# Edge features turned on the host, and gathers that read their row numbers in the table

## The chip, the cores and the metric

One core of a Trainium2 chip runs the whole program. The metric is device time in microseconds, the median of several runs. Times of single stretches come from one profiled execution.

## The reference, cut to what matters

Four graph layers over 3125 nodes and 100000 edges (sorted by destination), each followed by a layernorm. The change touches the second layer alone, its sum over the edges:

```python
src, dst = (edge_index[0], edge_index[1])
m_input = jnp.concatenate([node_states[src], node_states[dst], edge_rel_emb], axis=-1)
h = jax.nn.relu(m_input @ W1 + b1)
messages = jax.nn.relu(h @ W2 + b2)
agg = jax.ops.segment_sum(messages, dst, num_segments=node_states.shape[0])
updated = node_states + jax.nn.relu(agg @ Wn + bn)
```

`edge_rel_emb` is `edge_attr_64`, 64 numbers an edge.

## The kernel before

The edge loop takes the edges in 196 blocks of 512 (`BLK`, four columns of 128, `J` = 4), with four buffer slots (`SLOTS`). Ahead of it, fourteen steps project the node rows by the two halves of `W1` and store them in HBM as `xa_d` and `xb_d` (SP, lines 564 to 570; DVE copies them out at line 2029, into `proj(n)`).

For a block, in slot `v`:

- **POOL** (`gather`, line 730) issues four indirect DMAs, one for each 128 edges, that fetch rows of `xa_d` into `z_e[v]`. Each waits for its row numbers in a small table `idx` (semaphore `idx_ready`) and for the slot to be free (`z_ready` of the block four before). The first four blocks are written out, the rest run in a loop, the last block has a tail of its own (`last_gather`, line 739, two DMAs).
- **DVE** copies the row numbers of the block four ahead from the resident table `src_idx` to `idx` (`gather_index`, line 2013), adds a finished window of sums into the node sums (`add_window`), writes two one-hot tables for the block three ahead (`block_start`: line 2044 into the columns beside the features, line 2045 into `oh_e`), and adds the bias to the messages (`add_bias`, line 2049).
- **SP** (`edge_loads`, line 586) loads the features, 512 rows of 64, edges on partitions, into `ec` (`features`, line 553, after `ec_used` of two blocks before), and 24 rows of `xb_d` into `w_e` (line 590).
- **PE** turns features and one-hot columns (`inputs_t`, line 1027, four transposes), turns the gathered rows and adds the product of `w_e` and the turned inputs onto them (`hidden_t`, lines 1041 and 1045, which ends in `z_ready`), multiplies by `W2` (`messages`, line 1052) and sums messages by destination (`sum_nodes`, line 1061). In step `v` the order is: hidden of `v+1`, sums of `v-1`, inputs of `v+2`, messages of `v`.
- **ACT** copies the turned inputs out of PSUM into the one buffer `ec_t` (`inputs_out`, line 1478) and does the two relus (lines 1484 and 1488).

In five stretches of the loop the update of finished nodes is woven in (`blocks`, line 388), and in most blocks PE also adds a part of the next layer's sums (`partial`, line 1102).

## Time and profile before

| what | us |
| --- | --- |
| runs (three): median, lowest, highest | 1679.42, 1676.05, 1679.87 |
| the profiled execution, whole | 1675.27 |
| its span, first to last instruction | 1673.1 |
| PE busy | 1451.8 |
| POOL busy | 763.0 |
| DVE busy | 754.3 |
| ACT busy | 667.5 |
| the gathers in the edge loop (line 735), from and to | 489.7 to 1466.6 |

The time outside the span, 2.2 us, is the same work for any version. Busy times of different engines overlap; what a stage costs is read from the engine that the others wait for in that stage. Rows of the trace name the line, the engine, the tiles written and read, the time and, in brackets, the idle time ahead and what ended it.

### The profile page before, as it was taken

To read this page: it belongs to the slowest core of one execution; us is meant where nothing else is said; L and a number is where in the kernel's file an instruction comes from. 1 tells how busy PE (TensorE), PEld (TensorE's weight loads), DVE (VectorE), ACT (ScalarE), POOL (GpSimd) and SP (SyncE) were. 2 spreads that over 40 slices of the span, in tenths; PEclk is the share of its full clock that TensorE was granted. 3 is DMA by queue.
4 is the path that set the end of the run, shared out by engine and by line. 5 is a ranking of instruction groups with operands and counts; after the bars stand their busy time and mean duration, and the time that the engine had idled before them with its cause. 6 is when DMAs were issued, how large, how long until landed. Compare 5 with 4: busy or idle time off the path is not lost.

```text
span 1673.1 us, 30324 instructions
## 1 busy us (share of the span) xinstructions
PE 1451.8 (87%) x9336; PEld 1032.7 (62%) x9336; DVE 754.3 (45%) x2856; ACT 667.5 (40%) x1243; POOL 763.0 (46%) x806
## 2 busy tenths in 40 slices
PE   4899999999958777888989988998898889877997
PEld 3556666555556566666766766766666667654554
DVE  8799999513333222333243333333432343345445
ACT  6766666410023333443345334433443344331113
POOL 3000000000027777777777777777777777721000
PEclk9999999999978999999999998999899989988999
DMA  2000000020053333333333333333333333300001
GB/s 69 1 1 1 2 2 1 8 61 1 0 147 95 83 81 81 79 89 84 79 85 87 80 82 84 85 82 81 84 88 79 81 86 83 82 21 1 0 1 39
DMA packets 158120, 95.18 MB, mean 57 GB/s; under 512 B 119959, under 2 KB 143422, under 8 KB 158030
## 3 DMA queue, kind: packets, MB, share of 16 engines
q0 software_dynamic: 25024, 51.25, 12.0%
q1 hardware_dynamic: 133006, 42.78, 10.5%
q8 instruction: 50, 0.82, 0.2%
q14 instruction: 40, 0.33, 0.1%
HBM read 87.44 MB, written 6.52 MB: 56 GB/s over the span
## 4 chain that ended last, share of the span: by engine, by line
PE 31%; POOL 13%; DMA 11%; issue 9%; DVE 5%; ACT 1%; DVEq 1%; SPq 1%; POOLq 0%; ACTq 0%
POOL arena L735 13%; DMA arena<-x_w1a,idx 9%; PE ps L1167 6%; PE ps L1052 6%; PE ps L1061 5%; PE ps L1045 4%; PE ps L1041 3%; PE ps L1033 3%; PE ps L1102 2%; PE ps L1151 1%; DVE arena L2049 1%; DVE idx L2016 1%; DVEq L336 1%; DMA x_w1b<-arena 1%; DVE stats L2063 1%
## 5 line engine op out<-in xcount | busy, mean ns | idle before, releaser
L735 POOL DMA_INDIRECT arena<-x_w1a,idx x780 | 737.7, 946 | 713.3 <-issue 674.2
L1478 ACT ACTIVATE arena<-ps 88x512 f32<-88x512 f32 x196 | 116.2, 593 | 480.3 <-PE ps L1033 470.0
L1061 PEld LDWEIGHTS ps<-arena 128*128 128x128 f32 x1568 | 208.6, 196 | 111.5 <-issue 72.8
L2049 DVE TENSOR_TENSOR arena<-ps,bias_b 128x512 f32<-128x512 f32 x196 | 135.5, 691 | 208.0 <-PE ps L1052 208.0
L2044 DVE TENSOR_TENSOR arena<-win_i,late 128x96 f32<-128x96 f32 x196 | 50.8, 259 | 391.8 <-PE ps L1061 378.8
L1041 PE MATMUL ps<-ident_f,arena 128*128 128x128 f32 x784 | 130.1, 290 | 107.3 <-DMA arena<-x_w1a,idx 106.4
L1052 PE MATMUL ps<-w_c,arena 128*128 128x128 f32 x1568 | 222.6, 288 | 0.0
L1303 ACT ACTIVATE adj<-ps 128x300 f32 x392 | 171.0, 451 | 108.3 <-PE ps L800 103.8
L1045 PE MATMUL ps<-arena 88*128 88x512 f32 x392 | 208.0, 612 | 3.1 <-ACT arena L1478 3.1
L1052 PEld LDWEIGHTS ps<-w_c,arena 128*128 128x128 f32 x1568 | 205.9, 205 | 0.3
L1061 PE MATMUL ps<-arena 128*128 128x24 f32 x1568 | 197.9, 264 | 4.9 <-ACT arena L1488 1.4
L1041 PEld LDWEIGHTS ps<-ident_f,arena 128*128 128x128 f32 x784 | 91.1, 146 | 157.6 <-DMA arena<-x_w1a,idx 150.6
L795 PE MATMUL ps<-arena 128*128 128x300 bf16 x784 | 165.8, 294 | 25.2 <-DVE arena L1764 21.6
L1764 DVE TENSOR_SCALAR arena<-late,arena 128x300 bf16<-128x300 int16 x784 | 179.5, 292 | 0.0
L1484 ACT ACTIVATE arena<-ps,cols 128x512 f32<-128x512 f32 x196 | 134.6, 687 | 73.0 <-PE ps L1052 73.0
L844 PE MATMUL ps<-arena,adj 128*128 128x385 bf16 x625 | 151.7, 333 | 2.7 <-issue 2.7
L1033 PE MATMUL ps<-ident_f,arena 128*88 128x128 f32 x784 | 128.9, 290 | 25.7 <-DMA arena<-in_edge_attr 15.4
L795 PEld LDWEIGHTS ps<-arena 128*128 128x128 bf16 x784 | 85.0, 114 | 73.6 <-DVE arena L1764 26.1
L1488 ACT ACTIVATE arena<-arena 128x512 f32<-128x512 f32 x196 | 123.4, 630 | 11.2 <-DVE arena L2049 4.1
L800 PE MATMUL ps<-adj,ident_h 128*128 x392 | 122.9, 314 | 5.4 <-ACT adj L1303 3.8
L1167 PE MATMUL ps<-adj,arena 128*128 128x512 bf16 (+1 forms) x525 | 110.1, 364 | 8.8 <-DVE arena L2339 5.1
L1033 PEld LDWEIGHTS ps<-ident_f,arena 128*88 128x88 f32 x784 | 96.1, 152 | 28.6 <-DMA arena<-in_edge_attr 16.0
(205 smaller groups left out, 1406.7 us busy)
## 6 DMA issues: line engine op xcount, KB each, us to landing
arena<-in_edge_attr SPq DMA_DIRECT2D x196, 128.0 KB, 2.3
arena<-x_w1a,idx POOLq DMA_INDIRECT x782
arena<-x_w1b SPq DMA_DIRECT2D x196, 12.0 KB
x_spill<-arena SPq DMA_DIRECT2D x1, 1600.0 KB, 8.6
x_w1a<-arena SPq DMA_DIRECT2D x6, 256.0 KB, 2.3
x_w1b<-arena SPq DMA_DIRECT2D x6, 256.0 KB, 2.7
arena<-x_spill SPq DMA_DIRECT2D x6, 256.0 KB, 3.4
out_x<-arena SPq DMA_DIRECT2D x3, 512.0 KB
```

Source lines behind the costliest of these rows:

```text
L735: pool.indirect_dma_start(out=z_e[v][:, j * D:(j + 1) * D], out_offset=None, in_=xa_d[:, :], in_offset=bass.IndirectOffsetOnAxis(ap=idx[:, ...
L795: last = pe.matmul(ps[:, bank, 0:NT * WIN_A], oh_src[v][:, :, j], oh_dst[v][:, j, :], start=(j == 2 * h), stop=False)
L844: last = pe.matmul(ps[:, c1_bank(k), 0:3 * D + 1], adj[:, u, k * P:(k + 1) * P], mov_x[:, u, 0:3 * D + 1], start=(u == 0), stop=(u == NT - 1))
L1033: last = pe.transpose(ps[0:KE, 0, j * P:(j + 1) * P], ec[v % 2][:, j, :], ident_f[:, :])
L1041: pe.matmul(z_t[:, j * P:(j + 1) * P], z_e[v][:, j * P:(j + 1) * P], ident_f[:, :], is_transpose=True, start=(j == 0), stop=False)
L1045: pe.matmul(z_t, w_e[v % 2][0:KE, :], ec_t[0:KE, :], start=False, stop=True).then_inc(z_ready[v], 1)
L1052: last = pe.matmul(ps[:, 5, j * P:(j + 1) * P], h_t[:, j * P:(j + 1) * P], w_c[:, :], start=True, stop=True)
L1061: last = pe.matmul(ps[:, WIN_BANK[v % 2], 0:WIN], msg[:, j * P:(j + 1) * P], oh_e[v][:, j, :], start=(j == 0), stop=(j == J - 1))
L1167: last = pe.matmul(dst_bank(u), parts[q][:, k, :], adj[:, k, k0 * P:(k0 + nt) * P], start=((k, q) == (NT - 1, 0)), stop=(u != NC - 2 and ( ...
L1303: act.activation(adj[:, :, bass.ds(b, WIN_A)], ps[:, q % 4, 0:NT * WIN_A].rearrange("p (k w) -> p k w", w=WIN_A), ACT.Copy).then_inc(adj_w ...
L1764: last = dve.tensor_scalar(oh_dst[v][:, j, :], iota_c, comb[:, bass.ds(s, 1), j], None, ALU.is_equal)
L2049: dve.tensor_tensor(msg.rearrange("p (j d) -> p j d", d=D), bank(5, J), over(bias_b, J), ALU.add).then_inc(m_sum[v], 1)
```

## The change

The features come from the host turned (`attr_turned`, 64 rows of one number per edge), so that SP loads them straight into the rows of the matmul operand `ec_t`, of which there are now two. Into the 24 rows below, SP loads each edge's destination number, the same in all 24 rows (`dst_numbers`, int32), and DVE makes the one-hot rows there in place (`onehot_turned`): one compare of 24 x 512 against a column that holds the first node of the block plus the row's number (`first_nodes`). `inputs_t` on PE, `inputs_out` on ACT, and the one-hot columns of `block_start` on DVE are gone. `gather_index` and `idx` are gone too: POOL's 782 gathers are written out one by one, with no loop, and read their row numbers in `src_idx`. The features now wait for `z_ready` of two blocks before. In the first steps, DVE makes `first_nodes` where it copied four groups of row numbers.

```diff
         def features(i, v):
             e0 = (SLOTS * i + v) * BLK
-            passed(sp, ec_used, i, v, back=2)
-            sp.dma_start(ec[v % 2][:, :, 0:R],
-                         t["edge_attr_64"][bass.ds(e0, BLK), :].rearrange("(j p) f -> p j f", p=P)
+            passed(sp, z_ready, i, v, back=2)
+            sp.dma_start(ec_t[v % 2][R:KE, :].bitcast(I32),
+                         t["dst_numbers"][bass.ds(e0, BLK)].rearrange("(a e) -> a e", a=1).broadcast_to([WIN, BLK])
                          ).then_inc(ec_loaded[v], 16)
+            sp.dma_start(ec_t[v % 2][0:R, :], t["attr_turned"][:, bass.ds(e0, BLK)]).then_inc(ec_loaded[v], 16)
...
         def gather(i, v):
-            passed(pool, idx_ready, i, v)
             passed(pool, z_ready, i, v, back=SLOTS)
             pool.sem_inc(gather_mark, 1)
             for j in range(J):
                 pool.indirect_dma_start(out=z_e[v][:, j * D:(j + 1) * D], out_offset=None, in_=xa_d[:, :],
-                                        in_offset=bass.IndirectOffsetOnAxis(ap=idx[:, v, j:j + 1], axis=0)
+                                        in_offset=bass.IndirectOffsetOnAxis(ap=src_idx[:, SLOTS * i + v, j:j + 1], axis=0)
                                         ).then_inc(g_loaded[v], 16)
...
-            for v in range(SLOTS):
-                gather(0, v)
-            with pool.Fori(1, NB // SLOTS - 1) as i:
-                for v in range(SLOTS):
-                    gather(i, v)
-            for v in range(SLOTS - 1):
-                gather(NB // SLOTS - 1, v)
+            pool.wait_ge(words_moved, 48)
+            for n in range(NB - 1):
+                gather(n // SLOTS, n % SLOTS)
             last_gather(NB // SLOTS - 1, SLOTS - 1)
...
         def hidden_t(i, v):
...
-            passed(pe, ect_out, i, v)
+            passed(pe, ec_onehot, i, v)
             passed(pe, w_loaded, i, v, by=16)
-            pe.matmul(z_t, w_e[v % 2][0:KE, :], ec_t[0:KE, :], start=False, stop=True
+            pe.matmul(z_t, w_e[v % 2][0:KE, :], ec_t[v % 2][0:KE, :], start=False, stop=True
                       ).then_inc(z_ready[v], 1)
...
-            dve.tensor_tensor(ec[v % 2][:, :, R:KE], w, rel, ALU.is_equal).then_inc(ec_onehot[v], 1)
             dve.tensor_tensor(oh_e[v], w, rel, ALU.is_equal).then_inc(oh_e_ready[v], 1)
+
+        def onehot_turned(i, v):
+            passed(dve, ec_loaded, i, v, by=32)
+            rows = ec_t[v % 2][R:KE, :]
+            dve.tensor_scalar(rows, rows.bitcast(I32), first_nodes[:, bass.ds(SLOTS * i + v, 1)], None,
+                              ALU.is_equal).then_inc(ec_onehot[v], 1)
...
-        def step(i, v, b=None, left=3, first=False):
-
-            if left >= 3:
-                gather_index(*at(i, v + SLOTS))
+        def step(i, v, b=None, left=3):
+
             if b is not None:
                 add_window(*at(i, v - 2), b)
             if left >= 3:
-                block_start(*at(i, v + 3), first)
+                block_start(*at(i, v + 3))
+            if left >= 2:
+                onehot_turned(*at(i, v + 2))
             add_bias(i, v)
```

## Rows read from the trace of the kernel before

**Rows 1.** The page's chain that ended last, shares of the span by line.
```profile
POOL arena L735 13%; DMA arena<-x_w1a,idx 9%; PE ps L1167 6%; PE ps L1052 6%; PE ps L1061 5%; PE ps L1045 4%; PE ps L1041 3%; PE ps L1033 3%; PE ps L1102 2%; PE ps L1151 1%; DVE arena L2049 1%; DVE idx L2016 1%; DVEq L336 1%; DMA x_w1b<-arena 1%; DVE stats L2063 1%
```

**Rows 2.** Line 735: count, duration in ns (least/median/most), first and last start in us.
```profile
L735 POOL DMA_INDIRECT arena<-x_w1a,idx x780: 938/944/1217, 489.7 to 1466.6; - x195
```

**Rows 3.** Timeline of POOL, loop's start: start, duration in us, idle before in brackets.
```profile
489.67 1.13 POOL L735 DMA_INDIRECT arena<-x_w1a,idx  x1 [473.06 <-issue]
491.11 0.94 POOL L735 DMA_INDIRECT arena<-x_w1a,idx  x1 [0.31 <-issue]
...
511.51 0.94 POOL L735 DMA_INDIRECT arena<-x_w1a,idx  x1 [1.99 <-PE ps L1045]
...
517.61 0.94 POOL L735 DMA_INDIRECT arena<-x_w1a,idx  x1 [1.41 <-DVE idx L2016]
```

**Rows 4.** Waits, 540 to 1470 us: us in total, times, longest.
```profile
PE ps L1041 <- DMA arena<-x_w1a,idx: 106.4, 116, 1.8
```

**Rows 5.** The page's costliest groups: busy us, mean ns of one, idle before.
```profile
L1033 PE MATMUL ps<-ident_f,arena 128*88 128x128 f32 x784 | 128.9, 290 | 25.7 <-DMA arena<-in_edge_attr 15.4
```

**Rows 6.** The chain in order of time, ahead of the loop: start, us, what.
```profile
476.03 0.59 SPq L556
...
476.66 0.51 SPq L556
...
477.74 2.33 DMA x_w1a<-arena
```

**Rows 7.** Groups of DVE by line and shape: busy us, mean ns of one.
```profile
L1874 DVE TENSOR_SCALAR arena<-arena,mv,rstd 128x128 f32<-128x128 f32 x25 | 6.8, 340 | 0.1
L2008 DVE TENSOR_TENSOR arena<-arena 128x1024 f32<-128x1024 f32 x3 | 3.7, 1225 | 0.1
L1715 DVE TENSOR_SCALAR arena<-arena 128x784 int32<-128x784 int32 x1 | 0.6, 554 | 0.0
...
L2454 DVE TENSOR_SCALAR late<-ident_f 128x128 f32<-128x128 f32 x1 | 0.2, 219 | 0.0
```

**Rows 8.** Timeline, two copies of row numbers and the gathers that they meet.
```profile
930.21 0.95 POOL L735 DMA_INDIRECT arena<-x_w1a,idx  x1 [0.30 <-issue]
930.74 0.41 DVE L2016 COPY idx<-late 128x4 int32 x1 [1.21 <-issue]
...
1362.69 0.94 POOL L735 DMA_INDIRECT arena<-x_w1a,idx  x1 [0.30 <-issue]
...
1363.16 0.16 DVE L2016 COPY idx<-late 128x4 int32<-128x4 int32 x1
```

**Rows 9.** Timeline, a two-input operation of DVE and the longest gather of the loop.
```profile
1373.71 0.68 DVE L2117 TENSOR_TENSOR arena<-arena 128x512 bf16<-128x512 f32 x1
1373.99 1.22 POOL L735 DMA_INDIRECT arena<-x_w1a,idx  x1 [0.30 <-issue]
```

**Rows 10.** Timeline, a block's last gather, its transposes, the one-hot after them; two blocks.
```profile
871.26 0.95 POOL L735 DMA_INDIRECT arena<-x_w1a,idx  x1 [0.30 <-issue]
...
873.77 0.66 PE L1041 MATMUL ps<-ident_f,arena 128*128 128x128 f32 x4 [1.33 <-DMA arena<-x_w1a,idx]
...
876.13 0.26 DVE L2044 TENSOR_TENSOR arena<-win_i,late 128x96 f32<-128x96 f32 x1 [0.18 <-PE ps L1061]
876.26 0.95 POOL L735 DMA_INDIRECT arena<-x_w1a,idx  x1 [0.30 <-DVE idx L2016]
...
1001.43 0.94 POOL L735 DMA_INDIRECT arena<-x_w1a,idx  x1 [0.30 <-issue]
...
1004.24 0.66 PE L1041 MATMUL ps<-ident_f,arena 128*128 128x128 f32 x4 [0.32 <-DMA arena<-x_w1a,idx]
...
1006.71 0.26 DVE L2044 TENSOR_TENSOR arena<-win_i,late 128x96 f32<-128x96 f32 x1 [2.76 <-PE ps L1061]
```

**Rows 11.** Busy us by engine in two stretches of the loop, then granted clock, DMA.
```profile
540.00:600.00 60.00, 44.78 (x316) 36.30 (x315) 16.73 (x63) 24.15 (x38) 45.37 (x48) 1.00 0.34 84
...
1034.00:1044.00 10.00, 6.41 (x32) 5.63 (x32) 4.68 (x20) 3.19 (x6) 7.57 (x8) 0.67 0.49 121
```

More of the change, by code:

```diff
@@ L94, in build @@
         drel = late[:, J * (NB + 1):LATE].rearrange("p (s j) -> p s j", j=J)
-        base_row = sb("base_row", [1, NB], I32)
+        node_numbers = sb("node_numbers", [P, NB], I32)
+        base_row = node_numbers[0:1, :]
+        first_nodes = node_numbers[R:R + WIN, :].bitcast(F32)
         w_a = sb("w_a", [P, D], F32)
@@ L161, in edge @@
             return arena[:, a:a + n]
-        ec = [edge(J * KE * u, J * KE).rearrange("p (j f) -> p j f", j=J) for u in range(2)]
-        o = 2 * J * KE
+        ec_t = [edge(512 * u, 512) for u in range(2)]
+        o = 1024
         z_e = [edge(o + 512 * v, 512) for v in range(SLOTS)]
         h_t = edge(o + 2048, 512)
-        msg = edge(o + 2560, 512)
-        assert o + 3072 <= 3776
-        ec_t = edge(8000, 512)
+        msg = edge(8000, 512)
         w_e = [edge(9280 + 128 * u, 128) for u in range(2)]
@@ L261, in build @@
         ec_onehot = [sem(f"ec_onehot{v}") for v in range(SLOTS)]
-        ec_used = [sem(f"ec_used{v}") for v in range(SLOTS)]
         w_loaded = [sem(f"w_loaded{v}") for v in range(SLOTS)]
         oh_e_ready = [sem(f"oh_e_ready{v}") for v in range(SLOTS)]
-        ect_out = [sem(f"ect_out{v}") for v in range(SLOTS)]
         z_ready = [sem(f"z_ready{v}") for v in range(SLOTS)]
@@ L275, in build @@
         g_loaded = [sem(f"g_loaded{v}") for v in range(SLOTS)]
-        idx_ready = [sem(f"idx_ready{v}") for v in range(SLOTS)]
         gather_mark = sem("gather_mark")
@@ L1025, in _ @@
             pe.wait_ge(loads[6], 80)
-            def inputs_t(i, v, first=False):
-                passed(pe, ec_loaded, i, v, by=16)
-                if first:
-                    passed(pe, ec_onehot, i, v)
-                    passed(pe, ect_out, i, v, back=1)
-                for j in range(J):
-                    last = pe.transpose(ps[0:KE, 0, j * P:(j + 1) * P], ec[v % 2][:, j, :], ident_f[:, :])
-                last.then_inc(ec_used[v], 1)
             def hidden_t(i, v):
@@ L1071, in step @@
                     sum_nodes(*at(i, v - 1))
-                if left >= 2:
-                    inputs_t(*at(i, v + 2), first)
                 messages(i, v, first)
@@ L1197, in _ @@
             with pe.Else():
-                inputs_t(0, 0, first=True)
-                inputs_t(0, 1, first=True)
                 hidden_t(0, 0)
@@ L1473, in _, with hidden_relu @@
             act.wait_ge(loads[6], 80)
-            def inputs_out(i, v):
-                passed(act, ec_used, i, v)
-                passed(act, z_ready, i, v, back=1)
-                act.activation(ec_t[0:KE, :], ps[0:KE, 0, :], ACT.Copy).then_inc(ect_out[v], 1)
-            def hidden_relu(i, v, first=False):
-                if first:
-                    passed(act, z_ready, i, v)
+            def hidden_relu(i, v):
+                passed(act, z_ready, i, v)
                 passed(act, m_ready, i, v, back=1)
@@ L1490, in step @@
             def step(i, v, left=2):
-                if left >= 2:
-                    inputs_out(*at(i, v + 2))
                 if left >= 1:
@@ L1643, in _ @@
             with act.Else():
-                inputs_out(0, 0)
-                inputs_out(0, 1)
-                hidden_relu(0, 0, first=True)
+                hidden_relu(0, 0)
                 for v in range(SLOTS + 1):
@@ L2011, in _ @@
             phase_end(dve, 4)
-            def gather_index(i, v, first=False):
-                if not first:
-                    dve.wait_ge(g_loaded[v], 64 * i)
-                dve.tensor_copy(idx[:, v, :], src_idx[:, bass.ds(SLOTS * i + v, 1), :].rearrange("p a j -> p (a j)")
-                                ).then_inc(idx_ready[v], 1)
             dve.wait_ge(words_moved, 48)
@@ L2021, in _ @@
                                       base_all.rearrange("p (s a) -> p s a", a=1).broadcast_to([P, NB, J]), ALU.subtract))
-            for v in range(SLOTS):
-                gather_index(0, v, first=True)
+            own.add(dve.tensor_scalar(first_nodes, base_all[R:KE, :], part_i[R:KE, 0:1], None, ALU.add))
             for n, h, k0, nt in STEPS5:
@@ L2035, in _, with block_start @@
             base_regs = [dve.alloc_register(f"dve_base{v}") for v in range(SLOTS)]
-            def block_start(i, v, first=False):
-                if first:
-                    passed(dve, ec_used, i, v, back=2)
+            def block_start(i, v):
                 passed(dve, sums_ready, i, v, back=SLOTS)
@@ L2380, in _ @@
                 for v in range(3):
-                    block_start(0, v, first=True)
+                    block_start(0, v)
+                for v in range(2):
+                    onehot_turned(0, v)
                 dve.memset(agg_all, 0.0).then_inc(agg_zero, 1)
                 dve.wait_ge(agg_zero, 1)
-                step(0, 0, first=True)
+                step(0, 0)
                 step(0, 1)
```

12 lines of the change are left out of this document (7 added, 5 removed).

## The prediction, made before the changed kernel ran

> **What bounds the kernel now.** I read the chain that ended last first: its largest single line is POOL's gather, with the landing of gathers next [rows 1]. PE has the highest busy share of the page, so the question is whether PE or POOL sets the pace of the edge loop. The rows of line 735 answer it: 780 gathers of 0.944 us, started between 489.7 and 1466.6 us [rows 2]. That is 976.9 us for 779 steps, 1.254 us each; the timeline of POOL shows 0.94 us of work and 0.30 us of gap, 1.25 us, over and over [rows 3, 8]. POOL therefore hardly ever waits: the two stalls at the start, 1.99 and 1.41 us of gap where 0.30 is the rule, make 2.8 us, and what is left over 779 x 1.25 is about 1 us. PE, though, waits for the gathered rows 116 times in the loop, 106.4 us [rows 4]. So the loop is as long as POOL's chain: when the first gather starts, 782 steps, and a tail behind the last. In a block, four steps make 5.0 us.
>
> **What is taken off PE and ACT.** The four transposes of the inputs are 128.9 us of PE over 196 blocks, 0.66 us each [rows 5], and ACT loses a copy for each block. I cost both at a gain of nothing: the cover is POOL's chain. PE comes out 0.66 us earlier at the next gathered rows and waits there 0.66 us longer. If that cover were gone, so that PE set the pace, the same edit would be worth up to 128.9 us; the 116 waits speak against it.
>
> **POOL's own code.** Removed: the wait on the row numbers and the loop. The first sixteen gathers of the kernel before are already written out, and the second of them shows 0.31 us of gap and 0.94 us of work, as those inside the loop do [rows 3, 10]. The same goes for the step across a block, where the wait on the row numbers is named as releaser: 0.30 us too [rows 10]. I take 0 for all 782. Bounds: no loss larger than a hundredth of a microsecond a step shows anywhere, and a gain would have to come out of the 0.30 us, which the written-out gathers keep.
>
> **The loop's start.** Two edits meet here. SP issues four loads of features in place of two, ahead of the first store of projected rows, and this queue is on the chain: 0.59 and 0.51 us for the two, then the store at 477.74 us [rows 6]. Two more cost 1.1 us, and the first gather starts that much later (bounds 0, if the stores catch up, and 1.2). Against that, block 0 no longer passes through PE's transposes and ACT's copy, so its `z_ready`, for which POOL stalled 1.7 us beyond the usual gap, comes early enough; and the stall of 1.1 us on row numbers has no successor [rows 3]. I take -2.8 us (bounds 0 and -2.8). Net of the start: -1.7 us. Making `first_nodes` takes the place of four copies on DVE, while SP is on the chain: nothing.
>
> **SP's waits.** The features now wait for `z_ready` of two blocks before, with the 24 rows of `w_e` queued behind them, which wait for the same. They are needed a full block of PE work later than before, since the transposes are gone, so I cost the wait at nothing. In DVE's queue `onehot_turned` stands ahead of `add_bias`; its features were released a block earlier, so it should not wait except where SP is held by the node updates, five times, and there POOL has up to four blocks in hand.
>
> **What is added on DVE, and what it meets.** The compare of 24 x 512 has no twin in the trace, so I build its price. Single-input scalar operations of 4-byte numbers take 554 ns for 784 elements and 219 ns for 128: 0.51 ns an element, where a two-input operation takes 1225 ns for 1024 [rows 7]. With 512 elements that is 219 + 384 x 0.51 = 415 ns. One with two column operands takes 340 ns where one with none takes 219 [rows 7], so a column adds 60: 475 ns. DVE has room for it, being busy 16.7 of 60 us [rows 11], and saves 0.26 us of one-hot and 0.16 us of copy a block.
>
> But DVE and POOL get in each other's way. A copy that starts 0.47 us into a gather takes 0.16 us and the gather 0.94; one that starts at 0.53 takes 0.41 and ends with the gather, at 931.15 [rows 8]. So from about 0.6 us on, the gather holds something that this copy needs to write. The other way round, a two-input operation that is under way when a gather starts makes it the longest of the loop: 1.22 us, 0.27 longer, and it ends 0.40 us after the gather's start; the gather normally passes that point at about 0.13 [rows 2, 9]. Whoever is first keeps the other out until it ends. The copies are too short (four elements) to be seen holding a gather; the new compare, 0.475 us, is not.
>
> So its place in POOL's beat decides. The one-hot of line 2044, after which the compare will stand, started 4.87 us after a block's last gather in one block and 5.28 us in another [rows 10]. Less four steps, 5.0 us, that is -0.13 to +0.28 us into a gather. The compare starts when the one-hot (0.26 us) ends, at 0.13 to 0.54, and would end at 0.60 to 1.01. If it is under way at 0.6, the gather waits for its end: a delay of 0 at the early end, rising to 0.33 for a one-hot at +0.20; beyond that the gather is first, the compare waits, and POOL loses nothing. Evenly spread over the 0.41 us, the mean is 0.33 x 0.33 / 2 / 0.41 = 0.13 us. Since a late gather delays the rows and with them the next compare, the place in the beat stays the same and the loss comes back each block. PE waited for rows in 116 blocks; with 0.66 us less to do I take 150, and nothing for the rest: +19.5 us. Bounds: 0, and 196 x 0.33 = 65 us.
>
> The page "SBUF — State Buffer" of the Trainium skill, section "Who interferes with whom", says that VectorE in a two-port mode and GpSimd share a port pair as an exclusive lock, which whoever starts first holds for the whole instruction, and names `tensor_scalar` among the operations that take it. The rows agree on the lock but not on its length: a copy passes unharmed 0.47 us inside a gather [rows 8]. Were it held for the gather's whole 0.94 us, a compare that starts 0.13 to 0.54 into it would always be second, which is the first rival below.
>
> **The sum**, against the profiled execution: 1675.3 - 1.7 + 19.5 = 1693.1 us. The median of the runs lies 4.1 us above that execution, so I forecast 1697 us.
>
> **Rivals.** (1) *Not slower:* the gather is always first, and the compare falls behind it. It is decided by the compare's place: a start later than about 0.46 us into a gather (one-hot at more than +0.20), or before 0.13, and nothing is lost. The second block of [rows 10] would be such a one, and gathered rows that land a little later push all blocks there. Price: 1675.3 - 1.7 = 1673.6, as a median 1677.7. (2) *The upper end:* all blocks lock in at the worst place: 1673.6 + 65 = 1739, as a median 1743. (3) *Faster:* the 0.30 us between gathers is partly made by the wait and the loop. Each 0.05 us of it would give 782 x 0.05 = 39 us, 1639 as a median. The written-out gathers at 489.67 speak against it [rows 3]. (4) *PE's clock:* with 0.66 us less work a block, PE is idle more, and after a stretch in which it was busy 6.41 of 10 us the granted clock there read 0.67, between its full level and half [rows 11]. PE's work without the transposes is 44.78 / 12 - 0.66 = 3.07 us a block; at the half level 6.1, more than POOL's 5.0, or +1.1 x 196 = 216 us if it stayed. But at half level PE does not wait, and a busy PE got its clock back, so it should cost a lag that the slots take up. (5) The change not doing what it says would be POOL stalling on fetching its longer code; no row shows such a stall, and it would look like rival 2.
>
> **How the numbers follow.** The forecast case has 0.57, rival 1 0.25, rivals 2 and 5 0.07, rival 3 0.08, rival 4 0.03. A measurement of this kernel tells about 0.3%, 5 us, from no change. Rival 3 and a little of rival 1 are faster by more: 0.10. Most of rival 1, and a few weak cases of the forecast: same, 0.26. The rest is slower: 0.64. The range leaves out rival 3, rival 4 and most of rival 2: from 1672, rival 1 with the whole gain of the start kept, to 1728, where the mean delay is 0.25 us a block.
>
> **What would show it.** Right: gathers of line 735's successor at 0.944 us where the compare is not under way, and 1.05 to 1.25 us for one in four where it is, with the compare ending inside them; the gap staying 0.30 us; first gather near 490.8 us; no stalls of 2 and 1.4 us behind it; PE waiting longer for the rows. Wrong: all gathers at 0.944 us with compares stretched to a gather's end (rival 1); a gap other than 0.30 us (rival 3); long stretches at half clock with POOL waiting for `z_ready` (rival 4). The forecast fails too if the compare takes twice the 475 ns, as it would then not need what the copies need.

## The result, and the profile after

The changed kernel takes 1682.49 us (median of 16 runs, 1679.76 to 1684.37), the kernel before 1677.54 us beside it (16 runs, 1673.88 to 1680.6): ratio 1.0029, 95% interval 1.0021 to 1.0037. It is slower by some 5 us, where 19.5 - 1.7 = 17.8 us of loss had been forecast. The profiled execution has a span of 1678.9 us, 5.8 more than before.

The bound has not moved. The page's chain that ended last, by line, of the changed kernel; line 734 is the gather, 735 before [rows 1]:

```profile
POOL arena L734 25%; PE ps L1150 6%; PE ps L1030 5%; DMA arena<-x_w1a,late 4%; PE ps L1037 4%; PE ps L1046 3%; PE ps L1026 3%; PE ps L1085 2%; PE ps L1134 1%; DMA arena<-in_attr_turned 1%; DMA x_w1b<-arena 1%; PE ps L1154 0%; PE ps L1162 0%; PE ps L1013 0%; PE ps L1114 0%
```

The timeline of POOL at the loop's start (start, duration, idle before), against [rows 3]:

```profile
489.99 1.13 POOL L734 DMA_INDIRECT arena<-x_w1a,late  x1 [473.37 <-issue]
491.42 0.94 POOL L734 DMA_INDIRECT arena<-x_w1a,late  x1 [0.31 <-issue]
...
510.37 0.94 POOL L734 DMA_INDIRECT arena<-x_w1a,late  x1 [0.30 <-issue]
...
516.63 0.94 POOL L734 DMA_INDIRECT arena<-x_w1a,late  x1 [0.30 <-issue]
```

The two stalls are gone, the gap is 0.30 us as before, and in the whole loop no gap is above 0.32 us. What has changed is the gathers themselves. The group of POOL's gathers in the changed kernel (busy us, mean ns of one, idle before):

```profile
L734 POOL DMA_INDIRECT arena<-x_w1a,late x780 | 746.1, 956 | 710.8 <-issue 696.8 <-PE ps L1030 14.0
```

The same group of the kernel before, where the median was 944 ns [rows 2], as it still is:

```profile
L735 POOL DMA_INDIRECT arena<-x_w1a,idx x780 | 737.7, 946 | 713.3 <-issue 674.2 <-DVE idx L2016 37.1 <-PE ps L1045 2.0
```

746.1 - 737.7 = 8.4 us more in the gathers, -2.8 us for the stalls, +0.3 us for the first gather (489.99 against 489.67): +5.9, the 5.8 of the span. What follows the start of the last gather is the same, 203.9 us. These figures are of one execution of each kernel, which lies below its median by 1.7 us here and by 2.3 before.

The time above 944 ns, called the surplus below, is 9.7 us here and 1.3 before. Each long gather was matched with the VectorE operation that ends where it could go on: 52 of them with the new compare (6.2 us, of which 5.2 by compares under way when a gather begins), most others with two-input operations of the node updates (3.2 us, before 1.0). The pattern shows in single rows of the timeline. First, a compare that starts late in a gather and is under way when the next one begins; that gather is lengthened by 0.25 us:

```profile
734.68 0.48 DVE L2011 TENSOR_SCALAR arena<-arena,node_numbers 24x512 f32<-24x512 int32 x1
734.78 1.20 POOL L734 DMA_INDIRECT arena<-x_w1a,late  x1 [0.30 <-issue]
```

Second, two that start inside a gather: the one at 0.32 us costs nothing, the one at 0.44 us makes its gather end 0.1 us late:

```profile
1003.30 0.94 POOL L734 DMA_INDIRECT arena<-x_w1a,late  x1 [0.30 <-issue]
1003.62 0.48 DVE L2011 TENSOR_SCALAR arena<-arena,node_numbers 24x512 f32<-24x512 int32 x1
...
1008.29 1.04 POOL L734 DMA_INDIRECT arena<-x_w1a,late  x1 [0.30 <-issue]
1008.73 0.48 DVE L2011 TENSOR_SCALAR arena<-arena,node_numbers 24x512 f32<-24x512 int32 x1
```

Third, a block as the forecast had it, with a later place: its last gather, PE's transposes of its rows, and, 5.0 us behind that gather, the last gather of the next block, with the one-hot (line 2006) 0.24 us and the compare 0.53 us into it. The gather is first, and the compare takes 0.66 us:

```profile
1170.16 0.94 POOL L734 DMA_INDIRECT arena<-x_w1a,late  x1 [0.30 <-PE ps L1030]
...
1173.08 0.66 PE L1026 MATMUL ps<-ident_f,arena 128*128 128x128 f32 x4 [0.60 <-DMA arena<-x_w1a,late]
...
1175.20 0.94 POOL L734 DMA_INDIRECT arena<-x_w1a,late  x1 [0.30 <-issue]
1175.44 0.26 DVE L2006 TENSOR_TENSOR arena<-win_i,late 128x96 f32<-128x96 f32 x1 [1.07 <-PE ps L1046]
1175.73 0.66 DVE L2011 TENSOR_SCALAR arena<-arena,node_numbers 24x512 f32<-24x512 int32 x1
```

Fourth, one that starts 0.09 us ahead of a gather. The gather is first here too, although its record begins later: it keeps its 0.94 us, and the compare takes 0.55 us:

```profile
875.01 0.55 DVE L2011 TENSOR_SCALAR arena<-arena,node_numbers 24x512 f32<-24x512 int32 x1
875.10 0.94 POOL L734 DMA_INDIRECT arena<-x_w1a,late  x1 [0.30 <-issue]
```

Over the compares of this execution and of the eight experiments below that keep the instruction as it is (1752 in all), the place of the compare in POOL's beat of 1.25 us goes with the delay. Only gathers lengthened by the compare itself are counted; in the first row some 40 more are longer by up to 0.1 us (two by 0.14 and 0.18), each by the one-hot or a compare that was under way at the gather's start and ended 0.13 us and more into it:

| start of the compare in a gather, us | compares | held, taking over 0.5 us | gathers lengthened | mean delay over all of them, us |
| --- | --- | --- | --- | --- |
| 0 to 0.3 | 249 | 0 | 0 | 0 |
| 0.3 to 0.4 | 208 | 0 | 63 | 0.01 |
| 0.4 to 0.5 | 159 | 69 | 90 | 0.05 |
| 0.5 to 0.7 | 384 | 366 | 1 | 0.00 |
| 0.7 to 0.9 | 344 | 0 | 0 | 0 |
| 0.9 to 1.0 | 125 | 0 | 107 (the next) | 0.04 |
| 1.0 to 1.1 | 124 | 0 | 124 (the next) | 0.15 |
| 1.1 to 1.15 | 74 | 0 | 74 (the next) | 0.22 |
| 1.15 to 1.25 | 85 | 50 | 4 (the next) | 0.01 |

All 435 compares held in the rows from 0.4 to 0.7 us started between 0.46 and 0.69 us, and almost all ended 1.19 us after the gather's start. The 50 held in the last row started 0.05 to 0.10 us ahead of the next gather and ended 0.46 us into it, without delaying it; so no compare delayed a gather by more than 0.26 us.

PE waits about as often as before, 108 times against 116 [rows 4]. Its transposes of features are gone, but its clock is lower: 0.74 in the stretch of [rows 11] where it was 1.00, the mean of the execution 0.905 against 0.956, and the clock records of the loop show the half level (0.5) for 266 us, before for 99. PE's waits in the changed kernel, 540 to 1470 us (us in total, times, longest):

```profile
PE ps L1026 <- DMA arena<-x_w1a,late: 120.0, 108, 3.0
PE ps L1030 <- DVE arena L2011: 4.7, 4, 3.0
```

And its windows, with the columns of [rows 11]:

```profile
540.00:600.00 60.00, 52.39 (x261) 41.81 (x261) 18.71 (x48) 15.58 (x24) 45.37 (x49) 0.74 0.32 90
1034.00:1044.00 10.00, 6.54 (x45) 5.02 (x43) 5.21 (x18) 3.57 (x8) 7.56 (x9) 0.99 0.42 118
```

### The profile page after: what moved, and what is told of

Read it like the earlier page. It is cut to its first block, busy times and chain, and to the rows that moved or that the text cites. A ratio compares the mean times of both kernels' runs of the same rounds, so it can differ in the third digit from the quotient of the medians.

```text
span 1678.9 us, 28515 instructions
## 1 busy us (share of the span) xinstructions
PE 1448.6 (86%) x8467; PEld 1021.3 (61%) x8552; DVE 801.1 (48%) x2660; ACT 549.1 (33%) x1047; POOL 771.4 (46%) x807
## 3 DMA queue, kind: packets, MB, share of 16 engines
q0 software_dynamic: 25024, 51.25, 11.5%
## 4 chain that ended last, share of the span: by engine, by line
POOL 25%; PE 24%; issue 12%; DMA 5%; DVE 3%; SPq 1%; ACT 1%; POOLq 0%; DVEq 0%; ACTq 0%
POOL arena L734 25%; PE ps L1150 6%; PE ps L1030 5%; DMA arena<-x_w1a,late 4%; PE ps L1037 4%; PE ps L1046 3%; PE ps L1026 3%; PE ps L1085 2%; PE ps L1134 1%; DMA arena<-in_attr_turned 1%; DMA x_w1b<-arena 1%; PE ps L1154 0%; PE ps L1162 0%; PE ps L1013 0%; PE ps L1114 0%
## 5 line engine op out<-in xcount | busy, mean ns | idle before, releaser
L734 POOL DMA_INDIRECT arena<-x_w1a,late x780 | 746.1, 956 | 710.8 <-issue 696.8
L1046 PEld LDWEIGHTS ps<-arena 128*128 128x128 f32 x1568 | 232.7, 215 | 130.0 <-issue 78.7
L1037 PE MATMUL ps<-w_c,arena 128*128 128x128 f32 x1568 | 260.6, 317 | 0.0
L1026 PE MATMUL ps<-ident_f,arena 128*128 128x128 f32 x784 | 146.4, 317 | 131.1 <-DMA arena<-x_w1a,late 122.5
L1030 PE MATMUL ps<-arena 88*128 88x512 f32 x392 | 235.0, 685 | 5.6 <-DVE arena L2011 4.9
L1037 PEld LDWEIGHTS ps<-w_c,arena 128*128 128x128 f32 x1568 | 225.8, 221 | 0.5 <-issue 0.5
L1046 PE MATMUL ps<-arena 128*128 128x24 f32 x1568 | 218.8, 280 | 6.8 <-ACT arena L1463 4.4
L2011 DVE TENSOR_SCALAR arena<-arena,node_numbers 24x512 f32<-24x512 int32 x196 | 100.0, 510 | 24.3 <-DMA arena<-in_attr_turned 17.9
L927 PE MATMUL ps<-adj,arena 128*128 (+2 forms) x513 | 101.3, 356 | 0.6
L1733 DVE TENSOR_TENSOR arena<-late 128x512 bf16<-128x512 bf16 x196 | 82.4, 420 | 23.5 <-PE ps L789 22.3
```

The source lines that it names most:

```text
L734: pool.indirect_dma_start(out=z_e[v][:, j * D:(j + 1) * D], out_offset=None, in_=xa_d[:, :], in_offset=bass.IndirectOffsetOnAxis(ap=src_id ...
L1026: pe.matmul(z_t[:, j * P:(j + 1) * P], z_e[v][:, j * P:(j + 1) * P], ident_f[:, :], is_transpose=True, start=(j == 0), stop=False)
L1030: pe.matmul(z_t, w_e[v % 2][0:KE, :], ec_t[v % 2][0:KE, :], start=False, stop=True).then_inc(z_ready[v], 1)
L1037: last = pe.matmul(ps[:, 5, j * P:(j + 1) * P], h_t[:, j * P:(j + 1) * P], w_c[:, :], start=True, stop=True)
L1046: last = pe.matmul(ps[:, WIN_BANK[v % 2], 0:WIN], msg[:, j * P:(j + 1) * P], oh_e[v][:, j, :], start=(j == 0), stop=(j == J - 1))
```

## Experiments

The theory A to test: the loss is the compare on VectorE and the gathers on POOL holding each other up, by where the compare starts. Rivals: the written-out gathers and their reads of the resident table; the clock; the number of compares wherever they are. Ratios are to the kernel before, run on the same chip; "changed" is the changed kernel, 1.0029.

### Without the compare

```diff
-            passed(pe, ec_onehot, i, v)
+            passed(pe, ec_loaded, i, v, by=32)
...
-                if left >= 2:
-                    onehot_turned(*at(i, v + 2))
...
```

> The changed kernel without the compare on DVE: PE waits for the loaded rows themselves, and the 24 rows below the features hold destination numbers instead of a one-hot, so this part of the result is left out. Theory A (the compare and POOL's gathers keep each other out of a shared port): in the changed kernel the gathers' time beyond 0.944 us sums to 9.7 us over the loop, before to 1.3; without the compare it falls to about 3 us (what the two-input operations of the node updates cost) and the time to about 1676 us, 6.5 under the changed kernel and about 1.5 under the kernel before. Theory B (POOL's written-out code, or reading row numbers in the large table, costs the time) and theory C (the other shape of the feature loads does): the time stays at 1682.

1677.77 us, ratio 1.0002 (0.9991 to 1.0013), surplus 3.4 us:

```profile
L734 POOL DMA_INDIRECT arena<-x_w1a,late x780 | 739.7, 948 | 711.2 <-issue 695.4 <-PE ps L1030 15.8
```

Without the compare the loss is gone. The granted clock is no higher (0.898 against the changed kernel's 0.905), so the lower clock alone does not make the loss.

### Half the compare

```diff
-                rows = ec_t[v % 2][R:KE, :]
+                rows = ec_t[v % 2][R:KE, 0:BLK // 2]
...
```

> The changed kernel with a compare over 256 of the 512 columns; the other half of the one-hot rows is left out. Theory A, with the sizes read in the changed kernel's trace (a compare that ends more than 0.82 us into a gather, having begun before about 0.46, holds it up, and one that is still under way 0.13 us into the next gather holds that one up): the compare takes about 345 ns instead of 478, only those that begin later than 1.03 us into a gather still hold one up, so its share of the surplus falls from about 8 us to about 2.7, and the time to about 1677.5 us. A cost of the compare that does not hang on its length, or theories B and C: 1682.

1677.2 us, ratio 1.0004 (0.9994 to 1.0013). A compare takes 345 ns, the surplus is 4.2 us, of which compares make 0.7 in nine gathers (2.7 expected). Shortening it by 0.13 us takes nearly all of the loss away, not a quarter: a delay is what reaches over the point at which a gather cannot go on, and most reach over it by little.

### POOL's part alone

The kernel before, with written-out gathers that read `src_idx`, and no copies of row numbers (the diff's parts in `gather`, `gather_index` and the loop).

> The kernel before with one part of the change alone: the gathers written out, row numbers read in the resident table, no copies of them on DVE. Theory A: only the stall of 1.1 us on row numbers at the start goes, gathers stay at 0.944 us with 0.30 us between them: 1676.4 us against 1677.5 of the kernel before. Theory B: the whole loss is here, 1682 or more.

1674.53 us, ratio 0.9992 (0.9983 to 1.0001), surplus 1.7 us, gap 0.304 us. Writing the gathers out costs nothing. It is the lowest median of all, but cannot be told from the kernel before.

### The one-hot rows on ACT, behind the next relu

```diff
+            act.activation(rows, rows.bitcast(I32), ACT.Square, bias=first_nodes[:, bass.ds(SLOTS * i + v, 1)]
+                           ).then_inc(ec_apart[v], 1)
+            passed(act, ec_apart, i, v)
+            act.activation(rows, rows, ACT.Relu, bias=ones_c[R:KE, 0:1], scale=-1.0).then_inc(ec_onehot[v], 1)
...
                 if left >= 1:
                     hidden_relu(*at(i, v + 1))
+                if left >= 2:
+                    onehot_turned(*at(i, v + 2))
                 message_relu(i, v)
```

> The changed kernel with the one-hot made on ACT in two steps (square of the difference to the row's node, then relu of one minus it) in place of the compare on DVE. Theory A: ACT shares no port with POOL, so the gathers' surplus is about 3 us as without a compare, and the time about 1676 us, below both kernels. A rival to that: ACT, with about 1.2 us more in each 5 us block, becomes late for the messages and PE falls behind, but POOL has three blocks in hand, so this too should stay within 1 us. Theories B and C: 1682.

1887.5 us, ratio 1.126. The surplus fell as expected, to 2.3 us, but ACT's relu of block v+1 waits for PE's messages of v, so the one-hot behind it comes late and PE's product (line 1033) waits for it, and POOL for PE. The timeline of this kernel:

```profile
1001.10 0.71 ACT L1462 ACTIVATE arena<-arena,node_numbers 24x512 f32<-24x512 int32 x1
...
1001.85 0.72 ACT L1465 ACTIVATE arena<-arena,ones_c 24x512 f32<-24x512 f32 x1
...
1002.70 2.07 PE L1033 MATMUL ps<-arena 88*128 88x512 f32 x2 [1.55 <-ACT arena L1465]
...
1005.55 0.94 POOL L737 DMA_INDIRECT arena<-x_w1a,late  x1 [3.11 <-PE ps L1033]
```

PE's product takes 2.07 us here, where the granted clock is 0.50, the half level (1.02 us at the full one, in the changed kernel): this is the rival in which PE sets the pace, brought about by the order of ACT's queue. The expectation of within 1 us missed that.

### The same, first in ACT's step

Against the kernel of the section before:

```diff
+                if left >= 2:
+                    onehot_turned(*at(i, v + 2))
                 if left >= 1:
                     hidden_relu(*at(i, v + 1))
-                if left >= 2:
-                    onehot_turned(*at(i, v + 2))
                 message_relu(i, v)
```

> The one-hot rows are made on ACT in two steps (0.71 and 0.72 us), as in e4_act_compare, but they stand first in ACT's step, ahead of the relu of the next block, where ACT had 4.5 us of idle time. Theory A (the loss is VectorE's compare and the gathers holding each other up; e4's loss was the place in ACT's queue alone): POOL never waits for z_ready beyond the start, the gathers' time above 944 ns adds up to 2 to 3.5 us instead of 9.7, and the time is 1674 to 1678, about 5 us under the changed kernel. Rival B (two ACT operations a block are too much for PE's chain, or ACT's reads hold gathers up as VectorE's do): POOL gaps above 0.33 us in many blocks, or a surplus of gathers of 8 us or more, and 1683 us or more.

1676.76 us, ratio 1.0003 (0.9994 to 1.0012): as fast as the kernel before, with the features turned on the host. No gap of POOL is above 0.32 us. The surplus is 7.0 us, over the 2 to 3.5 that I had named, but one gather only (0.3 us) is matched with an operation of the one-hot; 4.5 us go to node updates that happened to lie at a costly place. The execution that was profiled is the slowest of this kernel's twelve (1680.49 us, 3.7 over the median), so its surplus says more than the kernel usually has, and the traces alone would show hardly any gain over the changed kernel (1680.8); that the loss is gone is shown by the medians. Work for the same rows on ACT leaves the gathers alone. A gather beside it in the timeline:

```profile
1003.16 0.95 POOL L737 DMA_INDIRECT arena<-x_w1a,late  x1 [0.30 <-issue]
1003.35 0.72 ACT L1462 ACTIVATE arena<-arena,node_numbers 24x512 f32<-24x512 int32 x1
...
1004.10 0.72 ACT L1465 ACTIVATE arena<-arena,ones_c 24x512 f32<-24x512 f32 x1
1004.41 0.94 POOL L737 DMA_INDIRECT arena<-x_w1a,late  x1 [0.30 <-issue]
```

### PE kept busy

```diff
                     sum_nodes(*at(i, v - 1))
+                if left >= 2:
+                    for j in range(J):
+                        pe.transpose(ps[:, 0, j * P:(j + 1) * P], ident_f[:, :], ident_f[:, :])
                 messages(i, v, first)
```

> The changed kernel with four transposes of the identity matrix in PE's step, where the removed transposes of the features stood (0.66 us a block, result not used). Theory A (half clock of a less busy PE moves the compare over the whole beat of POOL, and so into the read point of the next gather): PE's mean granted clock goes back from 0.905 to 0.94 or more, compares start mostly 0.3 to 0.6 us into a gather, the surplus of gathers that have a compare under way at their start falls from 5.2 to under 2 us, and the time is 1678 to 1681. The added work itself costs nothing, since POOL sets the pace. Rival B (the spread comes from when the rows land, not from the clock): surplus as in the changed kernel (9 to 11 us in all), 1682 to 1684. Rival C (PE's saved work was on the path after all): PE becomes the bound in part, POOL waits for z_ready, 1690 or more.

1680.24 us, ratio 1.0024 (1.0014 to 1.0035). The mean clock is 0.955 again, the half level 96 us of the loop, and 776 transposes more cost nothing. But compares are not gathered at 0.3 to 0.6 us: 37 of 196 start there, 51 in the changed kernel. Compares that reach over the next gather's start make 3.1 us, not under 2. A time inside A's interval, by another way: the rows were waited for in 145 blocks (115 in the changed kernel; this count takes in waits shorter than those of the view above), and there most compares start 0.5 to 0.9 us into a gather, where they delay none. The clock is at most a part of the spread, and the gain over the changed kernel is within both intervals.

### The compare as a two-input operation

```diff
-                dve.tensor_scalar(rows, rows.bitcast(I32), first_nodes[:, bass.ds(SLOTS * i + v, 1)], None,
-                                  ALU.is_equal).then_inc(ec_onehot[v], 1)
+                dve.tensor_tensor(rows, rows.bitcast(I32), first_nodes[:, bass.ds(SLOTS * i + v, 1)].broadcast_to([WIN, BLK]),
+                                  ALU.is_equal).then_inc(ec_onehot[v], 1)
```

> The compare as a two-input operation (the column broadcast as second input), about 0.69 us instead of 0.476. Theory A (any VectorE operation with its inputs in SBUF keeps the next gather from reading its row numbers until it ends): with the places in the beat that the changed kernel shows, compares that start later than 0.68 us into a gather hold up the next one by their place plus 0.69 less 1.374: 22 us in all where the changed kernel had 5 to 7, so about 1697 (1690 to 1706). Rival B (only the single-input form with a column of scalars takes what the gather needs): surplus of 3 to 4 us, 1677 to 1678.

1692.18 us, ratio 1.0095 (1.0082 to 1.0108), three times the loss. The surplus is 19.6 us; 82 gathers with 16.4 us go to the compare, all through the start of the next gather, and the delay is the place plus 0.69 less 1.374 within 0.03 us: 0.24 us for places of 0.9 to 1.0, 0.47 for 1.1 to 1.2. VectorE's group of it:

```profile
L2011 DVE TENSOR_TENSOR arena<-arena,node_numbers 24x512 f32<-24x512 int32 x196 | 134.2, 685 | 23.1 <-DMA arena<-in_attr_turned 16.9 <-issue 0.3
```

The timeline of one compare of this kernel, which costs 0.46 us:

```profile
1171.58 0.68 DVE L2011 TENSOR_TENSOR arena<-arena,node_numbers 24x512 f32<-24x512 int32 x1
1171.68 1.40 POOL L734 DMA_INDIRECT arena<-x_w1a,late  x1 [0.30 <-issue]
```

This form is never held inside a gather (685 ns is its own length; the 8 of 196 that took over 0.7 us started within 0.04 us of a gather's start), whereas the one-input form was, in 366 of 384 cases between 0.5 and 0.7 us. So the two forms meet a gather differently: both delay it at its start, only the one-input form meets it in its second half. The Trainium skill, page "SBUF — State Buffer", section "Who interferes with whom", says that a VectorE instruction with two inputs in SBUF contends with a GpSimd instruction that reads SBUF, and not with one that only writes it. The rows fit that, with 82 gathers lengthened at their start and none in the second half, if a gather reads its row numbers at its start and writes later; what a gather does when, no row shows.

### The features' part alone

The changed kernel, with POOL's loop, `idx` and the copies of row numbers as before.

> The features' part of the change alone: POOL keeps its loop, the wait for row numbers and the table of four blocks, and VectorE copies the row numbers as before. Theory A (the loss is the compare's): surplus of gathers 9 to 11 us, gap between gathers 0.30 us, 1682 to 1685. Rival B (the written-out gathers or their reads of the resident table cost what is lost): 1677 or less, as the kernel before.

1682.28 us, ratio 1.0036 (1.0023 to 1.0049). The features' part alone brings the whole loss. The surplus is 6.5 us and not 9 to 11; compares make 4.4 of it, and in this execution the first gather came 1.6 us later (491.6) and the tail took 2.8 us more (206.7) than in the changed kernel's; both vary by some 3 us between the executions of these kernels, with no cause that the record shows.

### The load of the destination numbers left out

```diff
-                sp.dma_start(ec_t[v % 2][R:KE, :].bitcast(I32),
-                             t["dst_numbers"][bass.ds(e0, BLK)].rearrange("(a e) -> a e", a=1).broadcast_to([WIN, BLK])
-                             ).then_inc(ec_loaded[v], 16)
...
-                passed(dve, ec_loaded, i, v, by=32)
+                passed(dve, ec_loaded, i, v, by=16)
```

> SP no longer loads the destination numbers into the 24 rows (one DMA a block less); the compare runs all the same on what stands there, so this leaves out the right one-hot rows. It asks why rows land later than before: with PE at full clock and waiting for rows, PE's transposes start 2.96 us after a block's last gather in the changed kernel, 2.78 before and 2.76 in e3_pool_only, which has the old features. Theory A (the load of the numbers, 24 rows of 2 KB, gets in the way of the gathers' packets): 2.76 to 2.85 us, places of the compare 0.1 to 0.2 us earlier, and a surplus that moves with them (8 to 15 us, 1682 to 1689). Rival B (the turned features, or the place of the loads in time, do it): 2.93 to 3.0 us, surplus and time as the changed kernel, 1680 to 1684.

1684.72 us, ratio 1.0042 (1.0028 to 1.0056). In blocks whose rows PE waited for at full clock, the transposes start 2.61 us (median) behind the last gather, against 2.96 in the changed kernel and 2.78 before: the load of 24 equal rows puts the landing of rows off by 0.35 us, more than the 0.1 to 0.2 expected. With the earlier landing, more compares come at 0.3 to 0.4 us, the place of the forecast, 50 of 196 where the changed kernel has 17. The surplus is 11.4 us, but 6.0 from compares, as in the changed kernel. In the 70 blocks that PE waited for at full clock they cost 2.2 us, 0.03 each: at the forecast's own place the loss is small too.

### Five attempts to fix the place

```diff
             def gather(i, v):
...
                 for j in range(J):
                     pool.indirect_dma_start(...
+                    if j == 1:
+                        pool.sem_inc(begun[v], 1)
...
+                if left >= 3:
+                    passed(dve, begun, *at(i, v + 3))
                 if left >= 2:
                     onehot_turned(*at(i, v + 2))
```

A mark is a semaphore that POOL raises and the compare waits for. One kernel raises it ahead of the four gathers, one behind the first of them (`j == 0`), one behind the second, as above; two more add two copies inside PSUM on VectorE between mark and compare.

> VectorE holds the compare of block v+2 back until POOL begins the gathers of block v+3 (a semaphore that POOL raises ahead of the first of the four), so that in the blocks whose rows PE waited for the compare no longer starts at a place of its own but always within 0.3 us before a gather. Nothing else changes. Theory A (the place in the beat decides the loss, through the point where a gather reads its row numbers): in about 110 of the 196 blocks the compare is under way when the gather reads them, 0.15 to 0.35 us of delay each, 16 to 38 us more surplus than in the changed kernel; 1693 to 1715, and the long gathers are the first ones of their blocks. Rival B (the loss goes with the number of compares, wherever they start): surplus stays at 6 to 10 us and the time at 1680 to 1685. Rival C (the wait keeps add_bias, queued behind it, and PE's sums late): POOL waits for z_ready, gaps beyond 0.33 us.

> As e9_at_mark, but POOL raises the mark behind the first of the four gathers, since in e9 the mark was up before the compare came (the compare waited 1.2 us in all). Now the compare of block v+2 should wait, in the blocks whose rows PE waited for, until the first gather of block v+3 has begun, and start 0.05 to 0.35 us into it, a place where neither held the other up in the changed kernel. Theory A (the place decides): of the compares of those blocks hardly any holds a gather up or is held (in the changed kernel 16 of 83 held one up, 24 were held), their part of the surplus falls from 1.2 us to under 0.4; the other blocks come late, find the mark up and keep their places and 4.9 us; 1679 to 1683. Rival B (the place has nothing to do with it): delays as before in number and size.

> As e11_after_first, with two copies inside PSUM on VectorE (about 0.7 and 0.25 us, not used) between the mark and the compare, so that the compare starts some 1.0 to 1.2 us into the gather and is under way when the next one reads its row numbers. Theory A: the delay is the place plus 0.476 less 1.374, 0.1 to 0.3 us, in the blocks that waited for the mark (some 80 to 110) and, since the copies shift the others as well, as before in those: 10 to 30 us more surplus than e11, 1690 to 1712. Rival B (the loss does not depend on the place): surplus as in e11, 1679 to 1685. Rival C (VectorE, 1 us longer in each block, holds up PE): POOL waits for z_ready, gaps beyond 0.33 us.

> The mark for the compare stands behind the second of the four gathers. In e11 the mark that stood behind the first gather went up 0.06 us into the gather before it, since POOL's sequencer is a gather ahead of POOL; so this one should go up 0.06 us into the first gather of block v+3, and the compares that come before it (those of blocks whose rows PE waited for, 60 to 120 of 196) start 0.1 to 0.2 us into it. Theory A (the place decides; a compare that starts up to 0.34 us into a gather and one that starts at 0.70 to 0.90 costs nothing): no gather held up by a pinned compare, no pinned compare held; the surplus that compares make falls from 5.7 us in e11 to 3 to 5, all of it by compares that were not pinned; 1678 to 1682. Rival B (the place has nothing to do with it): pinned compares hold gathers as often as others.

> As e13_pin_free, with the two PSUM copies of e12 (0.99 us together with their waits) between mark and compare, so that a pinned compare starts 1.05 to 1.2 us into a gather and is under way where the next one reads its row numbers, 0.13 us in. Theory A: each pinned compare holds the next gather up by its place plus 0.476 less 1.374, 0.15 to 0.25 us; with 60 to 120 pinned, 9 to 30 us more surplus than e13, 1688 to 1710: about the loss that the forecast put on every waiting block. Rival B: surplus and time as e13 within 3 us. Rival C (the longer VectorE step keeps PE's sums waiting): gaps of POOL beyond 0.33 us instead of longer gathers.

| kernel | us | ratio (interval) | surplus, of it by compares, us |
| --- | --- | --- | --- |
| mark ahead | 1682.68 | 1.0031 (1.0019 to 1.0043) | 10.4, 5.6 |
| mark behind the first | 1681.61 | 1.0031 (1.0019 to 1.0044) | 10.8, 5.7 |
| the same and two copies | 1684.06 | 1.0048 (1.0036 to 1.0061) | 9.4, 6.9 |
| mark behind the second | 1682.17 | 1.0036 (1.0023 to 1.0048) | 8.1, 5.2 |
| the same and two copies | 1684.31 | 1.0055 (1.0037 to 1.0074) | 10.1, 8.1 |

None fixed the place, so they don't decide between A and its rivals; by the times expected, the first and the two with copies came out as rival B had it. The reason is in the trace: the semaphore events of POOL's sequencer (its raising and waiting, which the profile keeps apart from POOL's work) stand far ahead of its gathers. With the mark ahead of the four gathers it goes up 11.5 us (median) before the first of them begins, with the mark behind the second still 10.0 us before the first. The compare hardly ever waits for it; VectorE's waits at line 2015 in the kernel with the mark behind the second gather, 540 to 1470 us:

```profile
DVE arena L2015 <- DMA arena<-in_attr_turned: 11.1, 5, 3.5
DVE arena L2015 <- issue: 1.2, 6, 0.4
```

The reading in my expectations, that the sequencer is one gather ahead, was wrong; it is nine. The copies moved the compares by 1 us, which is most of a beat, and left them spread. These kernels serve as repeats of the table of places. That the place could be fixed, and what the loss would then be, stays open.

## Why the prediction was right or wrong

**What bounds the kernel: right.** POOL's chain of gathers, nothing else; the 128.9 us of transposes taken off PE [rows 5] and a copy a block off ACT gave nothing. PE's wait for rows went from 106.4 to 120.0 us, and its busy time only from 1451.8 to 1448.6 us, at a mean granted clock of 0.905 in place of 0.956.

**POOL's own code: right.** Gap 0.304 us in both; POOL's part alone gives 0.9992. One row was misread: the gather at 876.26 us in [rows 10], with the row numbers named as releaser, is the last of its block and not a step across blocks. Of the 118 gathers so named in the kernel before, 4 are the first of a block: the sequencer waits far ahead, so the names stray. The gap across blocks is 0.30 us all the same.

**The start: right in its terms.** The four feature loads stand at 474.80 to 477.00 us in SP's queue, 1.1 us more than the two of [rows 6], and the two stalls of [rows 3] went. The first gather started 0.3 us later and not 1.1, because all of SP's queue ahead ran about 1 us earlier in this execution. That is no merit of the change: in the other kernels' executions the first gather starts anywhere from 488.7 to 491.7 us. SP's rows in the timeline of the changed kernel:

```profile
474.80 0.59 SPq L553 DMA_DIRECT2D arena<-in_dst_numbers  x1
475.43 0.47 SPq L556 DMA_DIRECT2D arena<-in_attr_turned  x1
475.94 0.55 SPq L553 DMA_DIRECT2D arena<-in_dst_numbers  x1
476.53 0.47 SPq L556 DMA_DIRECT2D arena<-in_attr_turned  x1
```

**The compare's length: right.** 476 to 479 ns where it is not held, against 475 built from [rows 7]; the group's mean of 510 holds the 0.2 us of those that are.

**SP's waits: right.** PE waited for the compare's rows 4 times, 4.7 us, and none of it reached POOL, which has no gap above 0.32 us.

**The mechanism: right in kind.** That the compare holds gathers up is shown by the kernels without it, with half of it, with it on ACT, and with it made longer: 1.0002, 1.0004, 1.0003 and 1.0095. But the way that the sum priced, a compare under way late in the same gather, brought only 1.0 us; the other 5.2 came through the start of the next gather, which the sum left out.

**The term of 19.5 us: the step that failed.** In its place stand 6.2 us by compares, 13.3 less, from three errors, which partly cancel. Of the 14.5 us between the forecast of 1697 and the 1682.5 measured, this is the bulk; another 2.4 are the distance of the median from the profiled execution, 1.7 us here where 4.1 was taken from three runs before.

First, the point. I took it that from about 0.6 us on a gather has to wait for any compare that is under way, since a copy that started at 0.53 was held [rows 8]. That is when VectorE is held. In the table's executions the gather is delayed only by a compare that ends later than 0.82 us into it, and one that starts from 0.46 to 0.69 is itself held. So the delay there is the place plus 0.476 less 0.82, at most about 0.1 us, not 0.33: two different points, read as one. In the 83 blocks of the forecast's case (rows waited for, full clock) the compares cost 1.25 us together, 0.015 each instead of 0.13.

Second, the place. The forecast let it stay within 0.41 us, in 150 blocks. Rows were waited for in 115 of the 196, and in 83 with the clock at its full level. In those the rows landed 0.18 us later than before, because of the load of the numbers, so the one-hot started 0.1 to 0.6 us into a gather and the compare behind the gather's point, as in the third rows above: 24 of the 83 were held and 67 delayed nothing. This is what rival 1 had said of later rows.

Third, the blocks that I set to nothing. In the other 113, PE is behind and catches up (81 of them did not wait for rows) or its clock is not at the full level, so the compares move over the whole beat. A part of them starts between 0.9 and 1.15 us and runs into the next gather, which the two-input operation of [rows 9] had already shown; I had used that row for the lock and not as a case. These blocks lost 4.9 us, 4.6 of it in this way. So only 1.25 of the 6.2 us come from the blocks that the sum was made for: that a loss came at all, as forecast, is for the most part luck.

**Rival 4** was half right: the clock stood at its half level for 266 us, but POOL had no gap above 0.32 us. Its price was a spread of places at most, which keeping PE busy did not do away with.

What stays open: 3.2 us of surplus by node updates, against 1.0 before. Their operations are the same; it was 0.5 us with POOL's part alone and 4.5 with the one-hot on ACT, and which of them meet a gather's start differs between the executions profiled, one of each kernel. The compare's place was never set on purpose either, so that the place makes the delay is read from where compares happened to fall.

## What to carry to other kernels

When operations of two engines hold each other up, find for each side the point at which it is held, from operations long enough to show it, and treat the two directions as two points: here VectorE is held if it starts 0.46 to 0.69 us into a gather, the gather only by a compare that ends beyond 0.82 us into it, or beyond 0.13 us into it from before its start. A step that meets a bounding engine costs by where it falls in that engine's beat, and the blocks that run late, not the regular ones, are those that sweep over the costly places. The same work on an engine that does not hold the bounding one up, as ACT here, is free (1.0003) if it stands in its queue ahead of what waits, and dear (1.126) if it stands behind.

## What the runs showed of the hardware

- POOL's sequencer ran some 11 us, nine gathers, ahead of POOL, so here a semaphore raised in POOL's program behind an indirect DMA told nothing of when that DMA was worked on.
- A gather of 0.944 us and the one-input compare of 0.476 us met in two places only. A compare that started 0.05 to 0.10 us ahead of the gather or 0.46 to 0.69 us into it was held (50 and 435 of 1752); one already under way delayed the gather when it ended beyond 0.13 us (begun before the gather) or beyond 0.82 us (begun inside it). All 593 that started at 0 to 0.3 or 0.7 to 0.9 us took their full speed and delayed nothing.
- Turning the features on the host cut the DMA packets from 158120 to 77372. The load of 24 equal rows of destination numbers a block raised the bytes from 95.2 to 104.8 MB, and gathered rows landed 0.18 us later than before; without that load they landed 0.17 us earlier than before.
